# Reordering the start-up, the clock's dummy matmuls and the last ranks of an RWKV-style attention with a mixture of experts

## What is computed

```python
# per channel, over the 64 time steps; p, q, o start at 0, 0, -inf
y = (A * p + E * vt) / (A * q + E)      # A = exp(o - no), E = exp(u + kt - no)
...
x = x + wkv(w, u, layernorm(x), ctx)
```

```python
h = layernorm(x)
probs = softmax(h @ gate_w);  w, sel = top_k(probs, 8);  w = w / sum(w)
...
y = (silu(h @ w_gate[e]) * (h @ w_up[e])) @ w_down[e]
x = x + sum over the chosen experts of w * y
```

## Time and profile before

| | us |
|---|---|
| median of 3 runs | 255.04 (254.72 to 255.62) |
| the profiled execution | 255.59 |
| its span, first to last instruction | 253.8 |

### The profile page before, as it was taken

One profiled execution on the slowest core, in us unless ns is written; L12 is line 12 of the kernel. 1 busy time (PEld: TensorE's weight loads), 2 busy tenths in 40 slices (PEclk: granted clock), 3 DMA queues, 4 the chain that ended last, 5 costly groups with the idle time before them and its releaser, 6 DMA issues.

```text
span 253.8 us, 4313 instructions
## 1 busy us (share of the span) xinstructions
PE 237.8 (94%) x1394; PEld 199.8 (79%) x1397; DVE 139.4 (55%) x359; ACT 132.0 (52%) x246; POOL 151.6 (60%) x141
## 2 busy tenths in 40 slices
PE   5559799999999999999999899999999999999993
PEld 2424799997888878889879688888888888888883
DVE  4697876993579647973985472242424242424243
ACT  2784759544894577558736513353535353535410
POOL 5145852258857794787686223386868686868630
PEclk9756999999999999999999999999999999999998
DMA  6951651000504333160505100003233232600002
GB/s 197 270 147 39 175 156 59 3 3 3 169 17 123 86 85 104 31 170 17 173 7 149 38 3 0 0 0 97 94 87 103 76 110 55 207 9 0 3 0 84
DMA packets 38414, 19.97 MB, mean 79 GB/s; under 512 B 29944, under 2 KB 38392, under 8 KB 38392
## 3 DMA queue, kind: packets, MB, share of 16 engines
q1 hardware_dynamic: 37544, 19.27, 26.4%
q10 hardware_dynamic: 848, 0.43, 0.6%
HBM read 18.65 MB, written 1.05 MB: 78 GB/s over the span
## 4 chain that ended last, share of the span: by engine, by line
PE 74%; DVE 9%; issue 6%; ACT 5%; POOL 4%; DMA 1%; DVEq 0%; POOLq 0%; ACTq 0%
PE bank L789 43%; PE bank L829 23%; POOL t_lo L427 2%; PE bank L844 2%; DVE t_sb L1224 2%; DVE t_sb L1218 1%; PE bank L810 1%; DMA x_sb<-in_x_dram 1%; PE bank L682 1%; PE bank L706 1%; ACT normed L511 1%; PE bank L691 1%; ACT t_hi L615 1%; POOL wlo L396 1%; DVE inv L1061 1%
## 5 line engine op out<-in xcount | busy, mean ns | idle before, releaser
L427 POOL TENSOR_TENSOR t_lo<-t_sb,t_hi 128x512 fp32r<-128x512 f32 (+1 forms) x53 | 62.0, 1169 | 74.5 <-ACT t_hi L615 71.6
L789 PE MATMUL bank<-h_hi,whi 128*128 128x512 f32 (+1 forms) x216 | 84.5, 391 | 0.3 <-DVE t_sb L1224 0.2
L396 POOL TENSOR_TENSOR wlo<-raw,whi 128x768 fp32r<-128x768 f32 x42 | 77.4, 1844 | 6.1 <-ACT whi L579 5.5
L789 PE MATMUL bank<-h_hi,wlo 128*128 128x512 f32 (+1 forms) x216 | 79.9, 370 | 0.0
L789 PE MATMUL bank<-h_lo,whi 128*128 128x512 f32 (+1 forms) x216 | 79.7, 369 | 0.0
L615 ACT ACTIVATE t_hi<-t_sb 128x512 fp32r<-128x512 f32 (+1 forms) x54 | 31.4, 582 | 83.1 <-DVE t_sb L1224 83.0
L1218 DVE TENSOR_TENSOR t_sb<-bank,s_sb 128x512 f32<-128x512 f32 (+1 forms) x54 | 34.0, 630 | 72.2 <-ACT s_sb L608 36.3
L829 PE MATMUL bank<-whi,t_hi 128*128 128x256 f32 x192 | 49.8, 291 | 0.1
L829 PE MATMUL bank<-wlo,t_hi 128*128 128x256 f32 x192 | 48.1, 282 | 0.0
L789 PEld LDWEIGHTS bank<-h_hi,wlo 128*128 128x128 f32 x216 | 40.6, 188 | 7.6
L789 PEld LDWEIGHTS bank<-h_hi,whi 128*128 128x128 f32 x216 | 41.1, 190 | 5.7 <-DVE t_sb L1224 0.4
(11 more groups left out here) (122 smaller groups left out, 182.3 us busy)
## 6 DMA issues: line engine op xcount, KB each, us to landing
raw<-in_L_ffn_w_gate_dram SPq DMA_DIRECT2D x14, 384.0 KB
raw<-in_L_ffn_w_up_dram SPq DMA_DIRECT2D x14, 384.0 KB
raw<-in_L_ffn_w_down_dram SPq DMA_DIRECT2D x42, 128.0 KB
out_dram<-x SPq DMA_DIRECT2D x4, 256.0 KB, 2.5
x_sb<-in_x_dram SPq DMA_DIRECT2D x1, 512.0 KB, 7.1
ctx_tile<-in_ctx_dram SPq DMA_DIRECT2D x4, 128.0 KB, 6.1
x_sb<-in_x_dram SPq DMA_DIRECT2D x1, 256.0 KB, 3.5
ctx_sb<-in_ctx_dram SPq DMA_DIRECT2D x1, 256.0 KB, 5.2
```

The source lines that it names most:

```text
L396: pool.tensor_tensor(split_view(wlo, slot, part), raw_parts(slot, part), split_view(whi, slot, part).bitcast(F32), ALU.subtract).then_inc( ...
L427: pool.tensor_tensor(t_lo[k % 2][:, c], t_sb[:, c], t_hi[k % 2][:, c].bitcast(F32), ALU.subtract).then_inc(t_lo_ready, 1)
L789: last = nc.tensor.matmul(ps[:, c], up_weight(w, slot, part, k, j), h[:, k, tokens], start=(i == 0), stop=(i == len(terms) - 1))
```

## The change

DVE makes the fractions of the denominators of a first pair right behind the scan of the keys, and scan and fractions of the values behind them; `begin_sums(second)` moves from ahead of `begin_refine(first)` to behind `mix(first)`, and `scan_keys(second)` from there to behind `stats_h(first)`. ACT inverts the first denominators ahead of `exps(second)`. POOL does `power(first, second_norm)` after one split instead of two. On TensorE three dummies become one and four around the wait for `inv_ready`, thirteen become six, two and two, the latter behind waits for `var_ready` and `rstd_ready`, and three become two. For the last tile TensorE's `ranks` go behind `down`. ACT fetches Silu's table behind `t_hi` instead of ahead of it.

```diff
@@ POOL
-            for part in range(2):
+            split_low(0, 0, 0)
+            power(first, first.second_norm)
+            for part in range(1, 3):
                 split_low(0, part, 0)
-            power(first, first.second_norm)
-            split_low(0, 2, 0)
@@ ACT
             exps(first)
             norm_x(second)
-            exps(second)
             begin_invert(first)
             end_invert(first)
+            exps(second)
...
-                        step(steps_before(half, it) + (p or 0) * TURN_STEPS + k, k, p, beside.get((p or 0, k), []), tiles and (lambda: tiles(it, k)),
-                             after.get((p or 0, k), []))
+                        step(steps_before(half, it) + (p or 0) * TURN_STEPS + k, k, p, beside.get((p or 0, k), []), tiles and (lambda: tiles[0](it, k)),
+                             [lambda: tiles[1](it, k)] if tiles else after.get((p or 0, k), []))
...
                     route_exps(routed)
+
+            def tiles_after(it, k):
+                at, back, _, _ = cycle(it, k)
+                if at == 2:
                     fetch_silu(back.n - 1)
@@ TensorE
                 turn_kv(u)
+            keep_clock(1)
             pe.wait_ge(inv_ready, 1)
-            keep_clock(3)
+            keep_clock(4)
             turn_mixed(first)
-            keep_clock(13)
+            keep_clock(6)
+            pe.wait_ge(var_ready, first.second_norm + 1)
+            keep_clock(2)
+            pe.wait_ge(rstd_ready, first.second_norm + 1)
+            keep_clock(2)
             turn_h(first)
-            keep_clock(3)
+            keep_clock(2)
...
-                elif at == (3 if front else 2):
+                elif at == 3 and front:
                     ranks(routed)
...
             def tiles_after(it, k):
                 at, _, routed, front = cycle(it, k)
-                if at == 1 and front:
+                if at == 2 and not front:
+                    ranks(routed)
+                elif at == 1 and front:
                     turn_kv(front)
@@ DVE
+            def fraction(u, i, done):
+
+                sl, per = u.slot, u.tiles * BPT
+                now, before = (num_ps, den_ps)[i][sl], state[sl][:, i]
+                dve.wait_ge(factors_ready, KT + 1)
+                chain.wait(done)
+                for k in range(KT):
+                    rows = slice(k * per, (k + 1) * per)
+                    last = nc.vector.scalar_tensor_tensor(out=now[:, rows, 1:], in0=now[:, rows, 1:], scalar=gain[:, k:k + 1],
+                                                          in1=before[:, rows, 0:S - 1], op0=ALU.mult, op1=ALU.add)
+                return last
+
+            def denominators(u):
+                fraction(u, 1, scan_keys(u)).then_inc(den_ready, 1)
+
+            def numerators(u, weighed):
+                chain.add(fraction(u, 0, scan_values(u, weighed)))
...
-            sums_done = sums(first)
-            fractions(first, *sums_done)
-            weighed = begin_sums(second)
+            weighed = begin_sums(first)
+            denominators(first)
+            numerators(first, weighed)
             begin_refine(first)
             end_refine(first)
             mix(first)
-            q_done = scan_keys(second)
+            weighed = begin_sums(second)
             add_mixed(first)
             stats_h(first)
-            p_done = scan_values(second, weighed)
-            fractions(second, q_done, p_done)
+            denominators(second)
+            numerators(second, weighed)
             h_low(first)
```

## The result

The changed kernel takes 253.53 us (median of 6 runs, 253.23 to 254.25) against 255.06 us for the kernel before, run beside it: ratio 0.9937, 95% interval 0.9923 to 0.9950, so 1.6 us (1.3 to 2.0) faster. I had forecast 252.9 and 2.1 to 2.4 us. The profiled execution took 253.34 us with a span of 251.6 us, against 255.59 and 253.8 before. That matters for most of what follows.

What follows compares the result with a forecast made beforehand. TensorE's own work bounds most of the span, leaving the start-up and the stall at 142.6 us. Start-up 1.03 plus ranks 1.33 gave 2.36 us; from 255.59 or 255.04 us this gave 253.2 or 252.7, forecast 252.9, own range 252.3 to 253.5.

Steps and rivals of the forecast that it cites:

- rival (a): Start-up: its gain does not arrive because ACT or POOL is late somewhere; 253.7 us, chance 0.16.
- The ranks: TensorE's stall at 142.6 us, last tile: `down` ahead of the ranks fills it; 1.33 us gained, between 0.8 and 1.36.
- slack of 0.8 us for `weigh_last`: Last tile: DVE's `weigh_last` is done 0.8 us before TensorE's turn of `wide` needs it.
- Part 1: Start-up, first pair on DVE and ACT: refining starts at 14.2 instead of 15.06, about 0.87 us earlier.
- Part 2: Start-up, from `mixed` to `h_lo`: another 0.16 us gained, `h_lo` starting at about 23.85 instead of 24.88.
- The dummies: TensorE's start-up: six, two and two neither hold `turn_h` nor leave more than 0.3 us free ahead of it.
- rival (d): Start-up on TensorE: with fewer dummies in three groups the clock rises late; slower, 257.3 us, chance 0.05.
- Part 4: ACT fetching Silu's table behind `t_hi`: 0 gained, between -0.1 and +0.4 us.

Runs made afterwards that it cites:

- kernel without new dummies: The changed kernel with TensorE's start-up dummies as in the kernel before (3, 13, 3): 253.28 us, again 253.52 us; ratios 0.9932 and 0.9938 to the kernel before.
- the fractions late: The changed kernel with the old dummies, the two fractions of the second pair's numerators moved from ahead of `h_low(first)` to behind `choose(first)`: 254.56 us.
- 21 dummies: The changed kernel with 11, 5 and 5 dummies in place of 6, 2 and 2 on TensorE between `mixed` and `normed`: 254.22 us, ratio 0.9951 to the kernel before.

## Why the prediction came out as it did

The measured 253.53 us lies in the wide range of 252.0 to 254.2 and just outside my own of 252.3 to 253.5. It is nearer to rival (a), 253.7 us, in which the start-up's gain does not arrive, than to the forecast of 252.9. What follows says which parts held.

**The ranks, 1.33 us: right.** 1.46 us by the traces (3.18 less 1.72), 1.2 us by the runs with an interval that holds 1.33. The 0.1 us above my upper bound of 1.36 is `down` itself: behind the stall it took 1.53 us (143.99 to 145.52), without it 1.43. The slack of 0.8 us for `weigh_last` measured 0.9.

**Part 1, the first pair: right, a little large.** 0.87 forecast, 0.77 measured from the weighing to the transposes of `mixed` (kernel without new dummies). ACT's inverse was early and DVE was the bound, as said. The term that was too small is the wait of a fraction for the scan just ahead of it. I took 0.04 from the refining pair; it is 0.10 to 0.11 each time (in the kernel after 10.01 + 1.22 to 11.34, and 21.44 + 1.21 to 22.75), 0.4 us in all four where I had booked 0.16.

**Part 2, `mixed` to `h_lo`: the step that failed.** I booked 0.16 us of gain from the earlier trace rows, where DVE idled 1.50 us ahead of `h_lo` because dummies held `turn_h`. That idleness was that of one execution, in which the clock rose at 23.3. With an earlier rise the same code has `h_lo` 0.4 us sooner (14.94 and 14.99 against 15.39), and the moved scan then costs 0.4 to 0.5 us instead of gaining 0.16. The start-up is worth about 0.3 us by the runs, at most 0.7, and not 1.03. I had written down this case under the sum (the median 0.5 us below the profiled execution because of the clock, only 0.4 to 0.5 us left, 253.2) and then set it half aside for 252.9. It was the right reading; the measured 253.5 is 0.3 above even that. The longer waits of the fractions, 0.25 us beyond what I booked, are of that size; no run tests them alone.

**The dummies.** The forecast was that six, two and two would never leave more than 0.3 us free. With the dummies alone, where the clock was low until 21.2 us, it nearly held: 0.34 and 0.52 us. At the full clock they left 1.12, 0.43 and 0.52 us, the clock fell, and the logits took 0.55 us longer. I had rival (d), a clock that rises late, with 2.6 us for logits and projections at half speed; what happened was an early rise and a fall, and most of its price disappeared behind DVE, for whose `wide` TensorE had been waiting 1.25 us anyway: here the projections end just as `wide` is there (28.74 to 29.00) and TensorE has no idle time left at that point.
The trace of before held a fall too, which I did not read; I wrote of one rise only. TensorE's timeline there:

```profile
7.80 0.71 PE L682 MATMUL bank<-ident,normed 128*128 128x128 f32 x4 [1.06 <-ACT normed L511]
...
11.14 1.13 PE L682 MATMUL bank<-ident,normed 128*128 128x128 f32 x4 [1.98 <-ACT normed L511]
```

Four such transposes take 0.71 us and then 1.13, and the granted clock is 1.00 up to 9 us, 0.84 from 9 to 10 and 0.50 behind that. So the record on hand already said that the clock can fall between short pieces of work.
The Trainium skill (TensorE: Matmul & The Clock Gate, section "A second HAM failure mode: psum-queue depth-cycling") says of another kernel that TensorE's short idle times between groups of matmuls come often enough to make the clock swing between its two levels. The traces agree as far as they go: the falls at 21.4 us here and at 30.3 us with the fractions late follow idle spells of 1.0 to 1.3 us.

**Part 4, Silu's table: right,** 0 forecast, +0.1 us (-0.3 to +0.4) measured.

**What the runs left open.** Why the clock rises at 15 us in both traces of the changed kernel and at 19.8 to 23.3 in the others that show a rise. The five dummies instead of three ahead of `mixed` are not reason enough: the kernel with the dummies alone and the one with 21 have them too, and rose at 21.2 in theirs. What tells these two traces from the rest is how long TensorE is idle between `turn_kv` and the dummies behind the wait for `inv_ready`. It is nothing and 0.35 us in the two with the early rise. It is 0.49 with 21 dummies, whose program is the same up to there, 0.59 to 0.93 in the others with the new order, 1.70 with the dummies alone and 1.96 with neither (before, ranks alone, Silu's fetch alone). By this both halves of the change would be needed, the dummy ahead of the wait and the earlier inverse, and even then the execution decides. No run tests it.
And a trace with 21 dummies and an early rise is missing, so that filling the gaps keeps the clock up is not shown.

## What to carry to other kernels

One profiled execution is one sample: where its own time differs from the median by as much as a term of your sum, find what makes it differ before that term is booked against it. When a chain is shortened by moving work on one engine into a gap, ask whether the gap belongs to the code or to that execution. And a wait that stands in order before independent work on the bound engine (the ranks ahead of `down`) is the cheapest thing to look for: it gave most of the gain for a few lines.

## What the runs showed of the hardware

The clock fell though TensorE was never idle for long: ahead of the fall at 21.4 us it had worked 2.57 of 4.40 us, and its longest idle spell since the rise was 1.31 us, 1.12 in the last 4.4 us. In the trace of before it fell at 9.7 us, where TensorE had been idle for 0.5 us and, since its first matmul, never longer than 1.06. I had thought of spells as a risk for the rise alone.

The recorded clock is not always what the matmuls ran at. In the second run of the kernel without new dummies the table by stretch shows 1.00 all along, and TensorE's timeline shows four transposes at 1.12 us, the length that goes with 0.50 in the other traces, and only from 22.7 us on the shorter one:

```profile
17.00:19.50 2.50, 2.47 (x8) 1.46 (x9) 1.93 (x6) 1.50 (x4) 1.36 (x1) 1.00 0.27 94
...
17.03 1.12 PE L695 MATMUL bank<-ident,mixed 128*128 128x128 f32 x4 [1.38 <-DVE mixed L1103]
...
22.73 0.75 PE L710 MATMUL bank<-ident,normed 128*128 128x128 f32 x4
```

So the mean clock of a run (0.97 to 1.00) says little of its start-up; lengths of known matmuls say more.

A dependent instruction on DVE starts 0.10 us behind the end of a scan, and 0.03 behind that of an elementwise product of the same size; the next independent scan starts some 0.09 us before the end of the one ahead (two in a row take 2.33 us, one alone 1.21).
